# Feed-forward phase: two output products of a group placed behind the first two expert halves of the next, and its first split placed ahead of the shared ones

## What is computed

```
shared = x2 @ sw1.T * sqrelu(x2 @ swg.T) @ sw2.T            # hidden width 256
xl     = x2 @ Wdown.T                                       # 128 wide
p      = sigmoid(x2 @ Wg.T), top 8 of 16 experts, scaled    # routing
acc    = sum over 16 experts of w[e] * ((xl @ rw1[e].T * sqrelu(xl @ rwg[e].T)) @ rw2[e].T)
out    = h + shared + acc @ Wup.T
```

## Time and profile before

| | |
|---|---|
| median of 3 runs | 2719.15 us (2715.58 to 2721.16) |
| the profiled execution | 2717.76 us, span 2715.9 us |
| TensorE busy | 2541.1 us, 94% of the span |
| ScalarE, Vector, GpSimd busy | 68%, 63%, 41% |
| TensorE's granted clock | 0.988 of full speed over the span |
| feed-forward phase | from about 1156 us to the end; a group takes about 95 us |

### The profile page before, as it was taken

How to read it: one execution, slowest core, us unless ns; L and a number is a source line. 1 busy time by engine, 2 the same in 40 slices (tenths; PEclk the granted TensorE clock), 3 DMA queues, 4 the chain that set the end, 5 groups by cost and what they waited for, 6 DMA issues and landing times.

```text
span 2715.9 us, 49409 instructions
## 1 busy us (share of the span) xinstructions
PE 2541.1 (94%) x13120; PEld 1883.0 (69%) x13120; DVE 1724.4 (63%) x3742; ACT 1838.5 (68%) x4597; POOL 1126.7 (41%) x1275
## 2 busy tenths in 40 slices
PE   3899999999999999969999999999999999999999
PEld 2566666666666666547878777877877787787787
DVE  5666666666666666357656765765576576557655
ACT  2666666666666666557766866876686677668666
POOL 3433333333333333214444544544464454436445
PEclk8999999999999999979999999999999999999999
DMA  3121212121211111142221222122122213212221
GB/s 100 32 64 62 62 62 63 62 62 62 62 62 62 62 62 46 45 146 90 98 87 50 94 86 86 47 98 86 52 92 88 84 46 100 85 53 89 89 69 60
DMA packets 99807, 197.67 MB, mean 73 GB/s; under 512 B 10928, under 2 KB 10928, under 8 KB 99568
## 3 DMA queue, kind: packets, MB, share of 16 engines
q1 hardware_dynamic: 94576, 179.29, 19.6%
q0 software_dynamic: 5120, 17.31, 2.8%
HBM read 128.89 MB, written 34.08 MB: 60 GB/s over the span
## 4 chain that ended last, share of the span: by engine, by line
issue 28%; POOL 24%; PE 2%; DVE 1%; ACT 1%; POOLq 1%; DMA 0%; SPq 0%; DVEq 0%; ACTq 0%
POOL t_lo L1147 22%; POOL sh_lo L1147 1%; POOLq L1145 1%; DVE ps_u L1516 0%; DVE f_lo L1541 0%; ACT x L1310 0%; DVE t L1523 0%; DMA x<-h 0%; ACT t_hi L1365 0%; PE fwork L1162 0%; PE ps_g L1162 0%; PE ps_u L1164 0%; PE ps_g L1164 0%; PE ps_u L1162 0%; PE ps_y L1162 0%
## 5 line engine op out<-in xcount | busy, mean ns | idle before, releaser
L1147 POOL TENSOR_TENSOR t_lo<-t,t_hi 128x512 fp32r<-128x512 f32 x512 | 664.6, 1298 | 437.2 <-ACT t_hi L1365 437.1
L377 POOL TENSOR_TENSOR probs<-probs,inv 128x512 f32<-128x512 f32 x256 | 265.3, 1041 | 626.6 <-DVE inv L774 626.4
L599 ACT ACTIVATE probs<-ps_s,nmax 128x128 f32<-128x128 f32 x1024 | 363.6, 371 | 222.4 <-DVE nmax L769 222.3
L1516 DVE TENSOR_TENSOR ps_u<-ps_u,square 128x512 f32<-128x512 f32 x512 | 357.3, 698 | 179.5 <-ACT square L1352 142.2
L1365 ACT ACTIVATE t_hi<-t 128x512 fp32r<-128x512 f32 x512 | 320.8, 627 | 129.4 <-PE ps_y L1164 72.6
L1523 DVE TENSOR_TENSOR t<-ps_u,w_all 128x512 f32<-128x512 f32 x512 | 354.0, 691 | 54.2 <-DVE ps_u L1516 18.4
L1348 ACT ACTIVATE square<-ps_g 128x512 f32<-128x512 f32 x544 | 320.5, 589 | 91.7 <-PE ps_g L1164 89.6
L1352 ACT ACTIVATE square<-square 128x512 f32<-128x512 f32 x544 | 344.4, 633 | 17.3
L488 PE MATMUL ps_s<-k_diag,qT 128*128 128x512 f32 x512 | 264.0, 597 | 0.0
L769 DVE TENSOR_REDUCE nmax<-ps_s 128x4 f32<-128x512 f32 x256 | 176.1, 688 | 102.3 <-PE ps_s L488 100.8
L1162 PE MATMUL ps_y<-t_hi,f_hi 128*128 128x512 f32 x512 | 209.9, 410 | 21.9 <-POOL t_lo L1147 21.6
(11 more groups left out here) (196 smaller groups left out, 5519.5 us busy)
## 6 DMA issues: line engine op xcount, KB each, us to landing
w_all<-w_rows SPq DMA_DIRECT2D x256, 256.0 KB, 3.2
res_next<-h SPq DMA_DIRECT2D x64, 256.0 KB, 2.3
res<-res_next SPq DMA_DIRECT2D x64, 256.0 KB, 2.3
h<-res SPq DMA_DIRECT2D x64, 256.0 KB, 2.0
x<-h SPq DMA_DIRECT2D x16, 1024.0 KB, 5.8
fres<-h SPq DMA_DIRECT2D x16, 1024.0 KB, 7.7
out<-fres SPq DMA_DIRECT2D x64, 256.0 KB, 2.3
fres<-in_w_ffn SPq DMA_DIRECT2D x14, 512.0 KB, 3.6
```

The costliest lines, as they stand in the source:

```text
L377: pool.tensor_tensor(probs[:, s % 4, :, :], probs[:, s % 4, :, :], inv[:, s % 4, :].rearrange("p (h o) -> p h o", o=1).to_broadcast([P, HP ...
L599: e = act.activation(probs[:, s % 4, j, :], ps_s[:, s % 2, j, :], ACT.Exp, bias=nmax[:, s % 4, j:j + 1], accum_out=total[:, s % 4, j:j + 1])
L1147: pool.tensor_tensor(lo, t[:, t_slot(j), :], hi.bitcast(F32), ALU.subtract).then_inc(t_lo_done, 1)
L1516: dve.tensor_tensor(dst, product, square[:, j % 2, :], ALU.mult).then_inc(t1_done, 1)
```

## The change

Two of a group's four output products (`LATE_OUT = 2`) are issued in the next group: output 2 behind the first products of its half 0, output 3 behind those of half 1. Vector's `add_out` of these two tiles moves along, behind `weigh` of half 0 and half 1. The accumulator's split moves from buffer 0 to buffer 1 of t_hi and t_lo, so that half 0 may write buffer 0 while outputs 2 and 3 are still due. ScalarE makes the copy of half 0 first and then those of the two shared units, all three behind the square of half 1; GpSimd follows in the same order, which `split_order` gives, and the waits on GpSimd's counter are rewritten with it. On SP the load of fres moves from ahead of `spread(g, 2)` to behind `spread(g, 4)`. In the last group all four outputs stay at the end.

```diff
+LATE_OUT = 2
...
-        acc_hi, acc_lo = t_hi[:, 0, :], t_lo[:, 0, :]
+        acc_hi, acc_lo = t_hi[:, 1, :], t_lo[:, 1, :]
...
+        def split_order(j):
+
+            return j + 1 if j < HC else 0 if j == HC else j
+
         def t_slot_left(g, j):
 
-            if j < HC:
-                return ALL_UNITS * (g - 1) + HC + UNITS - 2 + j + 1
             n = j - HC
-            if n < 2:
-                return ALL_UNITS * (g - 1) + HC + UNITS - T_SLOTS + n + 1
+            if n < 0:
+                return ALL_UNITS * (g - 1) + split_order(HC + UNITS - HC + j) + 1
+            if n < HC:
+                return ALL_UNITS * (g - 1) + split_order(HC + UNITS - T_SLOTS + n) + 1
             if n < T_SLOTS:
-                return ALL_UNITS * g + n - 2 + 1
-            return ALL_UNITS * g + HC + n - T_SLOTS + 1
+                return ALL_UNITS * g + split_order(n - HC) + 1
+            return ALL_UNITS * g + split_order(j - T_SLOTS) + 1
...
                 first = isinstance(g, int) and g == 0
-                if not first:
-                    load_res(g)
                 for e in range(2, EXPERTS):
                     spread(g, e)
+                    if e == 4 and not first:
+                        load_res(g)
...
-                pool.wait_ge(t_hi_done, ALL_UNITS * g + j + 1)
+                pool.wait_ge(t_hi_done, ALL_UNITS * g + split_order(j) + 1)
...
-                for j in range(ALL_UNITS):
+                for j in sorted(range(ALL_UNITS), key=split_order):
                     hidden_lo(g, j)
...
-                pe.wait_ge(t_lo_done, ALL_UNITS * g + HC + n + 1)
+                pe.wait_ge(t_lo_done, ALL_UNITS * g + split_order(HC + n) + 1)
...
                         first_products(g, n)
+                        if n < LATE_OUT and not (isinstance(g, int) and g == 0):
+                            output(g - 1, out_half(g - 1), TILES - LATE_OUT + n)
...
-                for i in range(TILES):
+                for i in range(TILES - LATE_OUT if more else TILES):
                     output(g, out_half(g), i)
...
-                    hidden_hi(g, HC + n - 1)
+                    if n == 1:
+                        hidden_hi(g, HC)
+                        hidden_hi(g, 0)
+                        hidden_hi(g, 1)
+                    elif n > 1:
+                        hidden_hi(g, HC + n - 1)
...
-                    hidden_hi(g + 1, 0)
...
                     linear(g, HC + n)
                     weigh(g, HC + n)
+                    if n < LATE_OUT and not (isinstance(g, int) and g == 0):
+                        add_out(g - 1, TILES - LATE_OUT + n)
...
-                for i in range(TILES):
+                for i in range(TILES - LATE_OUT if more else TILES):
                     add_out(g, i)
```

More of the change, by code:

```diff
@@ L1422, in _ @@
             weights_copy(0, 0)
-            hidden_hi(0, 0)
             group(0, True)
```

## The result

The change made the kernel slower: 2733.2 us median of 5 runs (2730.24 to 2734.16) against 2715.58 (2711.94 to 2721.16), a ratio of 1.0058 with an interval of 1.0043 to 1.0074. The forecast was 2711.6, and 2701 to 2722 as range; it started from 2719.15, the median of the three runs then known, so on the 2715.58 of all five its 7.5 us of gain would make 2708.1. The profiled execution after took 2730.24 us, span 2728.4.

What follows compares the result with a forecast made beforehand. TensorE, busy 94%, was taken as the bound, with a 1.22 us wait for t_lo at group starts. 13 edges × 0.59 = 7.7 us, less 0.2 for group 0, gave −7.5: from 2719.15 to 2711.6 us, range 2701 to 2722.

Steps and rivals of the forecast that it cites:

- (b): First t_lo of a group: with Vector's loop-edge pause staying 3.05 us, it comes 2 us early and the old pause goes.
- Rival C: Vector's loop edge gets dearer amid DMA traffic: from 0.84 us on the change loses; 2728 at 1.5 us; chance 0.15.
- (d): Load of x behind the four output stores: issued 2.76 us later, lands in 5.5 us, Vector's statistics stand 2.1 us.
- (e): Chain from x's landing through weigh(4), t_hi and t_lo to the fifth second product: gain 0.59 us per mean edge.
- (c): Second t_lo of a group, with t_hi[1] holding the accumulator until output 3 is done: TensorE pauses 0.2 to 0.6 us.
- The sum without the edge: Gain at the 13 edges inside the loop: 0.59 us each, 7.7 us; with the other terms −7.5 us together.
- the first change of group: Entry into the loop from straight code, with the shorter pause and x as late: 0 (−0.3 to +0.3) us.
- (f): Other moves: spread(2), no longer behind fres, arrives before weigh(4) even at 5.5 us; fres behind spread(4) delays nothing.
- Rival D: x lands within 4.7 us, so the second t_lo sets the time: gain 1.3 to 1.5 us per edge, 2699 to 2702; chance 0.15.

Runs made afterwards that it cites:

- e3: The changed kernel with the spreads of experts 0 and 1 moving only 16 of 512 columns from group 1 on: 2723.67 us, ratio 1.0017.
- e4 to e6: In turn: changed kernel with 64 memsets ahead on Vector, 2718.82 us; kernel before with Vector's loop cut elsewhere, ratio 0.9945; kernel before with the 64 memsets, 0.9952.
- e7: The changed kernel with x loaded ahead of the stores of tiles 2 and 3 and Vector's loop edge moved: 2695.77 us, ratio 0.9914.
- e2: The changed kernel with Vector's loop cut at another place, before the low part of the next group's latent: 2716.31 us, ratio 0.9991.
- e9: The changed kernel with Vector's loop edge moved and the load of fres back ahead of spread(2): 2754.81 us, ratio 1.0137.

## Why the prediction was wrong

**The step that failed** is (b), "If its pause stays (3.05 us from start to start ...)". The pause grew to 4.63 us (3.94 idle), 3.87 idle in the mean for 2.49. Nothing in the change touches what Vector does there; it moved the edge into the traffic of two spreads (e3: 0.8 of the 1.4 us by which the mean grew) and of the stores. In the traces the whole growth lies in the time until the packet of instructions starts, 1.90 us for 0.45, and not in what follows it; that the stores hold the part that e3 left is argued, not shown. Rival C was this case, with its cause, place and path right: some 0.25 us of cover, then one for one through add_out(3), the last store and x. I had put it at 0.15 on the ground that a whole extra microsecond shows nowhere. The trace of before had a sign of it: I took the longest pause, 2.9 us, for one beside quieter DMA, and it stood beside busier DMA (0.74 of the pause, for 0.30 at 1875). What I did not ask at all is why the edge costs anything; e4 to e6 show that it need not.

**The chain (d), (e) held.** It was forecast, 5.11 us added, as: add_out(3) at 1882.37, x issued at 1884.47, statistics at 1890.04, fifth second product at 1894.34. Measured: 1883.63, 1885.72, 1891.37, 1895.64. All are late by 1.25 to 1.33 us, the first delay and nothing else. x took 5.6 us for the 5.5 taken. So the stall did move to the fifth second product, and only its size was wrong. The 1.3 us of lateness turn the 0.59 us of gain into 0.7 us of loss, which is the mean of the twelve ordinary groups.

**(c) held in its number, by luck**: 0.39 us for 0.2 to 0.6. It had GpSimd start the two sh_lo when output 3 is done. With the change GpSimd works without a gap from the first t_lo, at 1882.52, to the second, which is ready near 1887.6; that start was set by the late weigh(0). Without the pause (e7) ScalarE's copies do wait for output 3, and TensorE still has no wait for the second t_lo: this wait, too, came from the edge.

**The sum without the edge** was 0.59 us per edge. e2, which has no extra pause, gained 0.0009 of before, 2.4 us in all, for the forecast's 7.5. By the transposes its 13 groups behind group 1 gain 6.3 us, or 0.48 each. The part missing is the first change of group, which I took as 0: x took 7.5 us to land there (the highest of the changed kernel's 14), and group 1 cost 3.8 us more than before with the change, nearly the same as in e2 (97.69 against 94.08 us). Some 1.7 us of it is the fall of TensorE's clock, a term that the forecast doesn't have.

**(f) was half right.** That fres away helps was right, by spread(2), and not by x as I had it in (d). "Even 5.5 would bring it before weigh(4)" hid how close it stands: weigh(4) had waited 0.93 us for this spread in the trace of before (at 1886.44), and e9 lost 1.4% of before.

**Rival D and the rule behind it** found no case: the shortest landing of x in any run here was 5.3 us. The Trainium skill (DMA: Bandwidth & Descriptors, Anatomy of one DMA, SWDGE (gpsimd) path) gives the rule for DMAs that GpSimd issues, and x is issued by SP; from it comes the estimate of 4.4 us for 1 MB, which the runs don't bear out here.

## What to carry to other kernels

Before work is reordered around a pause, ask what the pause is made of. Here a loop's edge on one engine was most of it, and shifting that loop in the instruction stream, by another cut or by 64 idle instructions, gave 0.5% with no reordering. The count of instruction packets on the page tells the two cases apart (91 against 27). An output that is finished later holds back every DMA that its queue has written behind it: put the loads that the next group waits for ahead of those stores. And when an edit shifts code ahead of or inside a loop, read the pause at the edge again; it can change by microseconds with no instruction of the loop changed in kind. Look at the granted clock behind every new stall of TensorE: here each fall cost an estimated 1.7 us beside stalls of 1.6 to 2.2 us.

## What the runs showed of the hardware that was not expected

Vector's pause at the back edge of a loop depends on where the loop lies in its instruction stream: 3.87 us, none beyond the 1.39 us wait for data with 64 more instructions in front, 3.82 us with 256; in the kernel before 2.49 us, and 1.38 us with 64 more. DMA traffic lengthens it: 3.06 us with most of two 256 KB spreads left out. In each of these pauses a packet of 8 KB starts on an instruction queue, and Vector goes on 1.96 to 2.28 us later; the rest is the time until the packet starts, 0.45 us in the mean before and 1.90 us with the change.

TensorE's granted clock fell from the upper to the lower level behind two waits of 1.15 and 1.05 us (0.67 in 1320 to 1325) and behind 0.59 and 1.05 us (0.83 in 2275 to 2285), but not behind 0.20 and 1.05 us, at 1893.63 and 1895.64.

A load of 1 MB took 5.7 us in the median to land whether 1 MB more stood 1.06 us behind it (e9) or not (e2), and 7.4 us with stores and a spread about it (e7); a 256 KB spread behind two such loads held its reader for 2.1 us.
